# Two packed attentions rewritten: each head in its own 32-row quarter of TensorE's array, one compact projection per side, the queries no longer spread by GpSimd

## The reference

```python
def _L1_xattn_ref(x, mask, kv, kv_mask, Wq, bq, Wk, bk, Wv, bv):
    q, k, v = (einsum('oc,bct->bot', W, src) + b)          # src is x for q, kv for k and v
    attn = softmax(where(kv_mask, (q * scale) . k, -inf))  # 16 heads, 256 x 256
    mean = attn . v;  std = sqrt(relu(attn . (v * v) - mean * mean))
    return (masked_instance_norm(x, mask) * std + mean) * mask
def _L3_xattn_ref(zt_prev, za, Wq, Wk, Wv, Wo, ...):
    q  = layer_norm(transpose(zt_prev + pos_enc))          # over the 128 channels
    kv = layer_norm(transpose(za + pos_enc))
    r  = softmax(Q . K / sqrt(8)) . V @ Wo + q
    return transpose(gelu(layer_norm(r) @ W1 + b1) @ W2 + b2 + r)
```

## Time and profile before

| | before |
|---|---|
| time, median of 3 runs | 2610.34 us (2607.75 to 2612.22) |
| the profiled execution's own time | 2606.17 us |
| its span in the trace | 2604.4 us |
| PE / PEld / DVE / ACT / POOL busy | 87% / 73% / 75% / 57% / 31% of the span |
| layer 1's attention, first scores to last moments | 1264 to 1640 us |
| layer 3's attention, start to last sum | 2160 to 2542 us |

### The profile page before, as it was taken

How to read it: one execution, slowest core, us unless ns; L and a number is a source line. 1 busy time by engine, 2 the same in 40 slices (tenths; PEclk the granted TensorE clock), 3 DMA queues, 4 the chain that set the end, 5 groups by cost and what they waited for, 6 DMA issues and landing times. The chain is left out here.

```text
span 2604.4 us, 53793 instructions
## 1 busy us (share of the span) xinstructions
PE 2273.9 (87%) x17161; PEld 1910.6 (73%) x17161; DVE 1945.2 (75%) x4994; ACT 1475.6 (57%) x4037; POOL 806.5 (31%) x978
## 2 busy tenths in 40 slices
PE   4999999977999999979788888499999696888886
PEld 4998989976989899969666666366666595777763
DVE  7666666677666666676699999788888665888866
ACT  3554555544555555557366566477777572666666
POOL 3011111120111111030344443466666303555530
PEclk7999999997999999989899999799999897999998
DMA  4000011000000100010000000100000000000000
GB/s 118 21 22 22 21 22 54 21 21 21 21 22 21 22 21 1 1 32 0 3 9 8 8 7 12 58 7 1 15 15 15 5 0 5 9 8 8 8 3 33
DMA packets 75321, 46.88 MB, mean 18 GB/s; under 512 B 31632, under 2 KB 74000, under 8 KB 75152
## 3 DMA queue, kind: packets, MB, share of 16 engines
q1 hardware_dynamic: 75152, 44.63, 6.6%
HBM read 41.46 MB, written 2.10 MB: 17 GB/s over the span
## 5 line engine op out<-in xcount | busy, mean ns | idle before, releaser
L2206 POOL TENSOR_TENSOR q_spread<-q_packed,part_of_head 128x512 fp32r<-128x512 f32 x256 | 262.5, 1056 | 371.9 <-DVE q_packed L1672 264.4
L1710 DVE TENSOR_REDUCE maxima<-bank 128x2 f32<-128x512 f32 x512 | 343.7, 681 | 34.7 <-PE bank L896 30.5
L1337 ACT ACTIVATE probs_t<-bank 128x512 f32<-128x512 f32 x512 | 286.4, 596 | 130.4 <-PE bank L886 128.0
L1242 ACT ACTIVATE wide_probs_t<-bank 128x256 f32<-128x256 f32 x256 | 98.3, 384 | 309.2 <-PE bank L762 306.9
L2101 POOL TENSOR_TENSOR wide_columns<-wide_pair_columns,zero 128x8 f32<-128x8 f32 x16 | 3.2, 202 | 858.3 <-DVE x L1590 815.4
L886 PE MATMUL bank<-q_spread,k_packed 128*128 128x256 f32 x1024 | 248.0, 326 | 5.2 <-ACT probs_t L1337 2.8
L896 PE MATMUL bank<-k_packed,q_spread 128*128 128x256 f32 x1024 | 214.7, 294 | 34.9 <-DVE maxima L1710 18.3
L1247 ACT ACTIVATE wide_probs<-bank,wide_neg_max 128x129 f32<-128x129 f32 x512 | 183.7, 364 | 85.5 <-DVE wide_neg_max L1560 81.0
L1254 ACT ACTIVATE wide_heads_high<-bank,wide_columns 128x128 fp32r<-128x128 f32 x512 | 159.9, 364 | 94.5 <-PE bank L774 93.2
L1565 DVE RECIPROCAL wide_inverse<-wide_sums 128x2 f32<-128x2 f32 x256 | 42.5, 166 | 224.0 <-ACT wide_probs L1247 224.0
L886 PEld LDWEIGHTS bank<-q_spread,k_packed 128*128 128x128 f32 x1024 | 168.1, 193 | 45.9 <-issue 28.1
(11 more groups left out here) (279 smaller groups left out, 6918.2 us busy)
## 6 DMA issues: line engine op xcount, KB each, us to landing
cn<-in_ctx SPq DMA_DIRECT2D x48, 128.0 KB, 2.1
wide_pair_weights<-in_L_xattn_wq SPq DMA_DIRECT2D x16, 256.0 KB, 2.9
wide_pair_weights<-in_L_xattn_wk SPq DMA_DIRECT2D x16, 256.0 KB, 3.3
wide_pair_weights<-in_L_xattn_wv SPq DMA_DIRECT2D x16, 256.0 KB, 3.8
wide_pair_weights<-in_L_xattn_wo SPq DMA_DIRECT2D x16, 256.0 KB, 3.5
wide_ctx_rows<-in_ctx SPq DMA_DIRECT2D x4, 512.0 KB, 4.7
x<-in_x SPq DMA_DIRECT2D x4, 512.0 KB, 5.6
wide_pair_rows<-in_L_xattn_bv SPq DMA_DIRECT2D x16, 128.0 KB, 4.0
```

The source lines that it names most:

```text
L1337: act.activation(probs_t[j % 8][:, :], shifted_bank[j % 2][:, :], ACT.Exp, bias=0.0).then_inc(s.exp_ready, 1)
L1710: dve.tensor_reduce(maxima[1 - u][:, j, :], head_scores[packed_scores(1 - u, j)][:, :].rearrange("p (a k) -> p a k", a=UNITS), X_AXIS, ALU ...
L2206: pool.tensor_tensor(q_spread[slot][:, first:first + SPREAD, :], q_packed[slot][:, pack:pack + 1, :].bitcast(F32).broadcast_to(wide), part ...
```

## The change

- **Quarters.** `q_packed` and `k_packed` keep one head per 32 rows: 8 rows each of three high/low pairings, and the two rows of the maxima. A head's products contract over its 32 rows alone (`quad[a]`), so no operand needs zeros, and `q_spread`, `part_of_head` and POOL's 256 multiplications are gone. In step j the shifted products take quarter j mod 4, the scores of the next batch quarter (j+2) mod 4.
- **Compact projections.** One f32 product of 256 columns per side (`w_queries`, `w_keys`) in place of four; ACT rounds to `q_high`/`k_high`, DVE subtracts to `q_low`/`k_low`, and four `put`s per window of four fp32r products each (L912) place them in the quarters with 0/1 matrices (`place`). ACT copies three of the four placed halves out of PSUM, DVE the first half of the keys; both keys' copies add the rows of ones.
- **Maxima.** DVE splits them before they are turned (128 x 16 elements, two linked instructions), TensorE turns the parts, DVE copies 32 x 128 out, SP issues four DMAs per half in place of two.
- **Work moved from DVE to POOL.** In layer 1 the masked keys, the values with their squares and the variance; in layer 3 the scaling of the normed inputs. ACT copies layer 3's turned inputs to SBUF first (`turned_packed`).
- **Order.** `over_batches` has windows from -5 to +1 around the batches, and a new table of steps (`Schedule`). The groups of sums stand at steps 3, 7, 11, 15 in place of 1, 5, 9, 13. The weights of layer 2 have SBUF of their own and load without waiting for the end of layer 1; the mask is widened row by row in layer 1 and no longer ahead of it.

The diff, cut to the core, TensorE's part first, then ScalarE's, VectorE's and GpSimd's:

```diff
-SCHEDULE1 = Schedule(turned=(3, 3), q=(7, 11), q_side=(0, 1), k=(12, 15), v=10)
-SCHEDULE3 = Schedule(turned=(3, 5), q=(12, 14), q_side=(1, 0), k=(11, 15), v=7)
+SCHEDULE1 = Schedule(place_k=0, project_k=2, turn=(6, 7), values=9, place_q_first=11, place_k_first=14, result=12)
+SCHEDULE3 = Schedule(place_k=1, project_k=3, turn=(6, 7), values=9, place_q_first=11, place_k_first=10, result=15)
+AHEAD, BEHIND = 5, 2
+PLACE_Q, PROJECT_Q = 0, 2
+TURN_MAXIMA = (9, 1)
+LAST_SUMS = 3
...
+                def put(name, half, bank):
+                    parts, base = ((q_high, q_low), 0) if name == "q" else ((k_high, k_low), 2)
+                    for m in range(2):
+                        for r, part in enumerate(parts):
+                            last = pe.matmul(bank[:, m * D:(m + 1) * D], place[:, base + r, 2 * half + m, :], part[:, :],
+                                             start=r == 0, stop=r == 1)
...
+                    b = (j + 2) % PACK
...
-                            last = pe.matmul(shifted_bank[j % 2][:, c * D:(c + 1) * D], k_packed[u][:, j // PACK, c * P:(c + 1) * P],
-                                             q_spread[u][:, j, :], start=True, stop=True)
+                            last = pe.matmul(shifted_bank[j % 2][:, c * D:(c + 1) * D], k_packed[u][quad[a], pack, c * P:(c + 1) * P],
+                                             q_packed[u][quad[a], pack, :], start=True, stop=True)
...
-                                             q_spread[1 - u][:, j, unit * P:(unit + 1) * P], k_packed[1 - u][:, j // PACK, :],
+                                             q_packed[1 - u][quad[b], pack, c * P:(c + 1) * P], k_packed[1 - u][quad[b], pack, :],
...
+                    if ahead and j == PROJECT_Q:
+                        pe.wait_ge(s.in_ready, n + 3)
...
+                        pe.matmul(upper[:, 0:D], w_q, source_q(at(2)), start=True, stop=True).then_inc(s.q_projected, 1)
...
+                    if third and coming and j == 13:
+                        pe.wait_ge(s.rows_normed, i + 4)
...
+                        act.activation(halves(q_packed[1 - u], 1), upper[:, :], ACT.Copy).then_inc(s.q_ready, 1)
...
+                        act.activation(halves(k_packed[1 - u], 1), lower[:, :], ACT.Identity, bias=ones_rows[:, 0:1]).then_inc(s.k_ready, 1)
...
+                chain.link(dve.tensor_copy(parts[:, :, 0, :], whole))
+                dve.tensor_tensor(parts[:, :, 1, :], whole, parts[:, :, 0, :].bitcast(F32), ALU.subtract).then_inc(s.max_split, 1)
...
+                        dve.tensor_scalar(k_packed[u][:, 0:2, :].rearrange("p g d -> p (g d)"), lower[:, :], ones_rows[:, 0:1], None, ALU.add)\
+                           .then_inc(s.k_ready, 1)
...
-                    chain.mark(dve.tensor_scalar(vn[u][:, c, :, 0:8], heads, valid_key, None, ALU.mult))
-                    chain.mark(dve.scalar_tensor_tensor(vn[u][:, c, :, 8:16], heads, valid_key, heads, ALU.mult, ALU.mult))
-                    ins = dve.tensor_scalar(vn[u][:, c, :, 16], ones[:, :], valid_key, None, ALU.mult)
...
+                        parts.mark(pool.tensor_tensor(v[:, c, :, 0:8], heads, of_heads, ALU.mult))
+                        parts.link(pool.tensor_tensor(v[:, c, :, 16], ones[:, :], valid_key.broadcast_to([P, HN]), ALU.mult))
+                        last = pool.tensor_tensor(v[:, c, :, 8:16], v[:, c, :, 0:8], heads, ALU.mult)
...
+                    chain.link(pool.tensor_scalar(scratch_keys, cn[1 - u][:, :], key_mean[:, 0:1], None, ALU.subtract))
+                    chain.link(pool.tensor_tensor(scratch_keys, scratch_keys, mask_row[:, 0, :], ALU.mult))
...
+                    pool.tensor_scalar(keys_in[1 - u], scratch_keys, key_mean[:, 0:1], None, ALU.add).then_inc(s.in_ready, 1)
...
-                        pool.tensor_tensor(q_spread[slot][:, first:first + SPREAD, :],
-                                           q_packed[slot][:, pack:pack + 1, :].bitcast(F32).broadcast_to(wide),
-                                           part_of_head[:, heads].unsqueeze(2).broadcast_to(wide), ALU.mult).then_inc(s.spread, 1)
...
+                    for k in range(4):
+                        ins = pool.tensor_scalar(norm_packed[:, k // 2, k % 2 * P:(k % 2 + 1) * P], turned_packed[:, k, :],
+                                                 stats.mean_var[:, k, 0:1], stats.rstd[:, k:k + 1], ALU.subtract, ALU.mult)
```

1031 lines of the change are left out of this document (493 added, 538 removed).

## The result

| | time, median | ratio to before, 95% interval |
|---|---|---|
| before, 7 runs | 2611.1 us | |
| the change, 7 runs | 2586.8 us (2579.2 to 2598.3) | 0.991 [0.989, 0.992] |
| forecast | 2514 us | 0.963 |

A forecast was written before the change was run, and what follows sets the result against it. Layer 1 was taken as bound by VectorE, layer 3 nearly by TensorE, which leads after the change. Savings of 66 and 30 us from the profiled 2606.2 give 2510, plus 4.1 for the median 2514 us; range 2460 to 2600.

The forecast's parts named there:

- TensorE's work: TensorE's summed work per window after the change: 16.3 us in layer 1, 17.6 in layer 3.
- The 0.24 for a step's products: Heads on TensorE: a step's four products overlap across quarters, 0.24 us; sixteen steps 3.8 us a window, before 7.5.
- a switch: TensorE changing its tiling: 0.17 us each, 25 a window in layer 1 and 27 in layer 3, 4.3 and 4.6 us.
- GpSimd late: Rival: GpSimd's results come 1.5 us late each time in layers 1 and 3, 45 us lost, 2559 us; chance 0.12.
- Both have nearly half a window, 9 us, for 5 to 7 us: Argument against GpSimd being late: its chains in layers 1 and 3 have 9 us for 5 to 7 us of work.
- the factor of 1.10: Window length over TensorE's work, from layer 3 before (21.4 for 19.4), applied to both layers: 17.9 and 19.4 us.
- 0.3 for VectorE close behind: Layer 1: 0.3 us a window added because VectorE at 16.0 us is near TensorE, giving 18.2.
- The ends of the layers are left as they are.: Fill and drain of the layers were taken as unchanged, adding nothing to the sum.
- The clock: Rival: lower clock for a quarter of layers 1 and 3; 21 us gained, 24 lost, 2613 us; chance 0.03.
- no overlap: Rival: products of two quarters wait for each other, heads stay at 7.5 us a window; 2631 us; chance 0.10.
- the 66 us forecast for layer 1's windows: Layer 1: 15 windows going from 22.6 to 18.2 us save 66 us.
- the 30 for layer 3's: Layer 3: 15 windows going from 21.4 to 19.4 us save 30 us.

The follow-up runs named there:

- run 2: The change with the second half's placements moved to step 1 and the projections to step 3, in both layers; 2575.9 us, 0.986.
- run 3: The change with shifted products and scores of a step in the same quarter of rows; 2749.5 us, 1.049.
- run 1: The change with layer 3's statistics one step earlier and aggregated at step 3 instead of 5 (the early statistics); 2548.0 us, 0.975.
- run 15: The change with run 1's early statistics and half of VectorE's reduction for the maxima left out; 2525.0 us, one execution timed.
- run 7: The change with layer 3's scaling of the normed inputs back from GpSimd on VectorE, at step 12; 2570.3 us, 0.985.
- run 10: The change with the edits of run 1 and run 7 together, early statistics and scaling on VectorE; 2567.5 us, 0.983.
- run 6: Run 1 with layer 1's values at step 10, first query placement at 12, and ScalarE's key rounding one step earlier; 2547.3 us, 0.976.
- run 9: Run 1 with second-half placements at step 1 and both projections at step 3, in layer 3 alone; 2548.1 us, 0.976.
- run 4: The change with each quarter product writing 128 of its 256 columns, the rest of each head's scores left out; 2640.6 us, one run.
- run 11: Run 1 with VectorE and ScalarE swapping which half of the placed keys they copy in layer 1; 2549.5 us, 0.976.

## Why the prediction was wrong

- **TensorE's work** was summed nearly right. Busy time per window of layer 1 is 130.67 / 150 x 19.3 = 16.8 us (forecast 16.3), and in layer 3 with early statistics 169.78 / 180 x 18.7 = 17.6 (17.6). Two parts were off against each other. The 0.24 for a step's products fits a lone step, 0.43 less 0.2 for the way in and out; in a pair two steps cost that together, so the heads are cheaper than the 3.8 summed. And a switch costs about 0.2 (0.1 for the products that must end, 0.1 for a load that is not made ahead), not 0.17. By the Trainium skill's page "TensorEngine Tiling (Array Packing)", Key Properties, a change of mode drains the array; the 0.1 on leaving the quarters agrees. Not every change shows it: in run 2 a product in a 32-column strip (L905, 1427.14) follows one over all columns (L912, 1427.03) after 0.11 us, as without a change. The rule of the Trainium skill's page "TensorE: Matmul & The Clock Gate", Part 3, that a load overlaps products only in another row group, does not fit run 3, where the third and fourth product of one quarter follow at 0.12.
- **GpSimd late: the step that failed, as run 1 shows.** "Both have nearly half a window, 9 us, for 5 to 7 us" was wrong for layer 3 on both sides. The rows of before had the roots right (5.3 us), but no row priced the scaling on GpSimd, and the text never added it: 0.79 us for each of four, 3.15, so the chain is 8.7 us long. And it has 6.5 us in place of 9: it starts at 2367.0, when VectorE has aggregated, and TensorE came to step 13 at 2373.5; the chain ends at 2375.7. The rival had the mechanism, 1.5 us and 0.12; measured are 2.1 us a window (19.1 / 9) in layer 3 and none in layer 1. Run 1 takes it away and layer 3 comes to 18.7, better than the 19.4 forecast.
- **Layer 1** came to 19.3 and not 18.2 because the factor of 1.10 was borrowed from layer 3; it is 19.3 / 16.8 = 1.15. The "0.3 for VectorE close behind" was 0.75 by run 15.
- **"The ends of the layers are left as they are."** They were not. Against 15 windows (15 x 19.3 = 290) layer 1 takes 40 us more than its windows, before 31; and the way from the feed-forward into layer 3 grew from 24.2 to 32.8 us. That is not the clock, which was low there before too (0.58 and 0.55). GpSimd is busy for 16.1 us of it, before for 6.8; with the scaling on VectorE the way takes 27.7 us (run 7), with early statistics as well 26.3 (run 10), so most of it is GpSimd's chain. What the deeper pipeline (windows from -5 on in place of -2) costs beside it was not tested.
- **The clock** was put at nothing in the sum, and given 0.03 as a rival, on the ground that TensorE idled for 16% and 11% before without a fall. The mean granted clock of whole executions went from 0.956 to 0.932. The steady windows kept it (0.99 in layer 1, 0.96 in layer 3), but layer 3 as a whole went from 0.99 to 0.86 and spent over a quarter of its time at the lower level, the share that the rival had assumed. What it costs there is seen against run 1: 10.7 us of busy time behind the windows and 6.4 in them. The gains of runs 2, 6 and 9 were lost beside it in their profiled executions. What makes it fall is not shown by any run.
- **Right:** quarters overlap (run 3, the "no overlap" rival), VectorE at 78% of layer 1 (forecast 88, of a shorter window), 16.3 us of work (16.8 measured), layer 2 untouched (361.9 us against 362.0).

In all, of the 66 us forecast for layer 1's windows 49 came, of the 30 for layer 3's about 1. From these 50 go 9 at layer 1's ends, 11 between the layers and 16 in layer 3's first and last windows, where the clock was 0.58 and 0.76, and 5 that were of the one execution: 9 are left, as its span shows. So the ends took 36 us, somewhat more than the 29 missing in layer 3's windows, and they are the part that is only partly explained.

## What to carry to other kernels

Moving work to an idle engine needs a date and not only a share: add up the whole chain on it, from the instruction that starts it to the step at which the result is due. The busy shares of GpSimd here (28% of the span) said nothing of its being 2 us late in each window, and moving the start of its chain by two steps gained more than the rewrite. Where small tiles alternate with full ones, count visits: a lone step of four small products costs as much as eight.

## What the runs showed of the hardware that was not expected

- Two loads of one quarter at the entry into a tiling follow each other by 0.106 us, and 0.22 us lie between the first two products; from the third on a product every 0.117 us, in the same quarter too.
- Products of four quarters given one after the other ran at the same time, eight in 0.43 us, whichever of the two orders they were given in.
- Less work for TensorE was slower in run 4 (0.74 granted from 1360 to 1600, TensorE busy for 90%), and the clock was 0.65 in run 3 in a stretch busy for 95%. The waits ahead of the falls in runs 2 and 9 stand in other windows without a fall. So idle time is not the whole of it; what the small products contribute stays open.
- GpSimd's scaling of 128 x 128 elements with two scalars of a column each took 0.79 us, VectorE's 0.41 (L2027).

The fastest versions that leave nothing out are run 1 and three built on it (runs 6, 9 and 11), at 0.975 to 0.976; the simplest of them is run 1.
